# A four-layer graph network on one core: f2's column computed inside the values' matmuls, its maximum taken through a 32x32 transpose, and ScalarE's work in layer 0 in another order

## The reference

```
layer 0, 3 (GAT):  Wh = h @ W;  f1 = Wh @ a1;  f2 = Wh @ a2
                   e[n,m] = leaky_relu(f1[n] + f2[m], 0.2), masked; softmax over m
                   out = elu(attention @ Wh) in layer 0, relu(...) in layer 3
layer 1:           a softmax per channel over the neighbours, weights from softplus(h)
layer 2:           4 heads: scores h_head @ h_head.T, masked softmax, times h_head;
                   then one such attention on the joined heads, leaky_relu, layernorm
```

## Time and profile before

| what | value |
|---|---|
| median of 3 runs | 1895.6 us (1892.89 to 1895.61) |
| the profiled execution | 1894.35 us, its span 1892.1 us |
| busy in the span | PE 97%, PEld 81%, DVE 88%, ACT 68%, POOL 48% |
| layer 0 | about 31 to 245 us of the span |
| layer 1 | about 245 to 406 us |
| layer 2 | about 406 to 1731 us (the first units of layer 3 lie inside its end) |
| layer 3 | to the end |

### The profile page before, as it was taken

How to read it: one execution, slowest core, us unless ns; L and a number is a source line. 1 busy time by engine, 2 the same in 40 slices (tenths; PEclk the granted TensorE clock), 3 DMA queues, 4 the chain that set the end, 5 groups by cost and what they waited for, 6 DMA issues and landing times.

```text
span 1892.1 us, 92007 instructions
## 1 busy us (share of the span) xinstructions
PE 1840.0 (97%) x42280; PEld 1531.0 (81%) x42280; DVE 1660.6 (88%) x1932; ACT 1285.1 (68%) x2052; POOL 907.5 (48%) x686
## 2 busy tenths in 40 slices
PE   7999899999999999999999999999999999999998
PEld 6887799987878788787888878878787878877887
DVE  6989899768898889988899888989988899888998
ACT  4998676446777777777777777777777777754332
POOL 6888999633233343424344342443334334264753
PEclk8999999999999999999999999999999999999999
DMA  7000000012111112221111211111111112201111
GB/s 192 4 4 4 3 2 3 2 25 36 37 36 36 36 36 37 34 38 31 36 34 35 38 34 36 36 36 36 36 37 36 36 35 32 42 3 26 26 32 31
DMA packets 134321, 61.02 MB, mean 32 GB/s; under 512 B 122416, under 2 KB 122672, under 8 KB 133936
## 3 DMA queue, kind: packets, MB, share of 16 engines
q1 hardware_dynamic: 131712, 54.55, 14.3%
q10 hardware_dynamic: 2224, 0.59, 0.1%
HBM read 8.98 MB, written 4.19 MB: 7 GB/s over the span
## 4 chain that ended last, share of the span: by engine, by line
PE 84%; POOL 8%; DVE 4%; issue 2%; ACT 1%; DMA 0%; ACTq 0%; POOLq 0%; DVEq 0%
PE ACC L1914 30%; PE S L1895 29%; PE S L1872 8%; PE ACC L1712 7%; PE AX L1957 3%; PE AX L1930 2%; DVE ring L1336 1%; PE AX L1702 1%; PE AX L1692 1%; POOL above L643 1%; PE S L1769 1%; POOL o L639 1%; DVE ring L1484 1%; PE AX L1753 1%; POOL X L649 1%
## 5 line engine op out<-in xcount | busy, mean ns | idle before, releaser
L1484 DVE TENSOR_TENSOR ring<-ring,mask_self_t 128x1024 f32<-128x1024 f32 x640 | 878.0, 1385 | 68.8 <-ACT ring L1092 61.1
L1092 ACT ACTIVATE ring<-S,dot_bias 128x1024 f32<-128x1024 f32 x640 | 711.5, 1113 | 274.3 <-PE S L1895 235.7
L1914 PEld LDWEIGHTS ACC<-V,ring 128*64 128x64 f32 x20480 | 706.7, 138 | 109.8 <-issue 13.2
L1914 PE MATMUL ACC<-V,ring 128*64 128x65 f32 x20480 | 708.0, 222 | 0.0
L1895 PE MATMUL S<-FA 128*64 128x512 f16 x5120 | 665.5, 380 | 1.1 <-ACT ring L1092 0.9
L1895 PEld LDWEIGHTS S<-FA 128*64 128x64 f16 x5120 | 268.6, 110 | 141.8 <-issue 10.9
L1336 DVE SCALAR_TENSOR_TENSOR ring<-S,pair_q,mask_t 128x1024 f32<-128x1024 f32 x256 | 313.9, 1273 | 16.5 <-issue 4.3
L1712 PEld LDWEIGHTS ACC<-V,ring 128*64 128x64 f32 x8192 | 253.3, 139 | 56.2 <-DVE ring L1336 34.7
L1712 PE MATMUL ACC<-V,ring 128*64 128x65 f32 x8192 | 270.4, 225 | 20.3 <-DVE ring L1336 11.5
L819 POOL TENSOR_TENSOR EV_both<-score,recip 128x512 f32<-128x512 f32 x64 | 96.8, 1512 | 263.9 <-DVE score L1494 263.8
L1872 PE MATMUL S<-parts,mask_t 128*128 128x128 bf16 x3072 | 173.8, 220 | 4.7 <-DVE o L1461 3.5
(11 more groups left out here) (149 smaller groups left out, 2076.6 us busy)
## 6 DMA issues: line engine op xcount, KB each, us to landing
FA<-FA SPq DMA_DIRECT2D x160, 128.0 KB, 2.3
X<-in_x SPq DMA_DIRECT2D x16, 256.0 KB, 4.8
ring<-in_adj SPq DMA_DIRECT2D x8, 512.0 KB, 8.1
out_x<-X SPq DMA_DIRECT2D x16, 256.0 KB, 2.6
FA<-HL SPq DMA_TRANSPOSE x80, 3.1
wh<-in_wh_t ACTq DMA_DIRECT2D x2, 64.0 KB, 6.5
bh_bc<-in_bh ACTq DMA_DIRECT2D x1, 128.0 KB, 9.9
w_gat<-in_w_gat ACTq DMA_DIRECT2D x4, 16.0 KB, 3.9
```

The lines of the kernel that those rows point to most:

```text
L1092: act.activation(ring[:, jt, :], S[jt % 2][:, :], ACT.Exp, bias=dot_bias[:, n % 2:n % 2 + 1])\
L1484: dve.tensor_tensor(ring[:, jt, :], ring[:, jt, :], mask_self_t[:, jt, :], ALU.mult)\
L1914: last = pe.matmul(acc_of(t)[rows, :], ring[:, jt, t * P + c * CUT:t * P + (c + 1) * CUT], V[:, n % 3, jt, 1:D + 2], start=(jt == 0 and t ...
```

## The change

Seven things are changed.

1. `w_gat` holds W a2, then W, then W a1. One group of matmuls of 65 columns for each tile gives f2 and the values together (`gat_columns`); `gat_peak` and its 32 instructions a unit are gone. The group stands where `gat_peak` stood: for unit cur+2, after tile 2 of cur.
2. ScalarE copies the 65 columns to V (`gat_columns` on ScalarE), now for unit cur+2. V has four buffers in place of three. VectorE's `node_max` waits for this copy and reads f2 from V, no longer from PSUM.
3. The maximum over partitions starts with a 32x32 block transpose on VectorE: f2 and norm2 are 32 columns wide, of which 8 are used; copy, transpose, maximum over 32 columns, each waiting for the one before. So only 32 partitions' values need to be spread: the two matmuls of `spread` have 32 columns in place of 128, and `node_peak` and `bias` read 32 in place of 128. This holds for layer 0, 2 and 3 (`norms` and `bias` too).
4. A round of ScalarE in layer 0 becomes: copy ACC of cur-1, h_relu of cur+2, exponents and gain of cur+1, columns of cur+2, late_shifts, gat_below of cur-1, late_squares.
5. For the last two graphs of layer 0 the ELU is max(exp(min(o,0))-1, o): GpSimd makes the minimum, ScalarE one exponent in place of two passes, VectorE one instruction (`gat_elu`), GpSimd adds once in place of twice.
6. In layer 3 the same order without the means; the two buffers of the first three units are chosen anew.
7. Three memsets and one wait at the start, and four small copies of `w_gat` in place of two.

The diff, cut to its core:

```diff
+    SQ = 32
...
-        V = sb("V", [P, 3, T, D + 2])
+        V = sb("V", [P, 4, T, D + 2])
...
-            return 2 * ((b + layer // 3) % 2)
+            return (0, 1, 2)[b % 3] if layer == 0 else (2, 3, 0)[b % 3]
...
+        ELU_SWITCH = B - 2
...
# GpSimd
+                if layer == 0 and b >= ELU_SWITCH:
+                    wait(pool, elu_made, b)
+                    pool.wait_ge(gat_o, n + 1)
+                    pool.tensor_scalar(below[:, :], o[:, :], 0.0, None, ALU.min).then_inc(elu_below, 1)
...
+                if layer == 0 and b >= ELU_SWITCH:
+                    pool.wait_ge(elu_made, b + 1)
+                    pool.tensor_tensor(x_of(b), x_of(b), tiles(o[:, :]), ALU.add).then_inc(x_done[layer], 1)
...
# ScalarE
-                act.activation(halves_of(V[:, buf, :, 1:D + 1]), V_FULL, ACT.Copy).then_inc(gat_v_copied, 1)
+                act.activation(halves_of(V[:, buf, :, 0:D + 1]), V_GAT, ACT.Copy).then_inc(gat_v_copied, 1)
...
                     for k in steps_beside(cur):
                         channel_argument(k, k % 2)
+                    if cur + 1 < B:
+                        gat_factors(layer, cur + 1)
+                    if cur + 2 < B:
+                        gat_columns(layer, cur + 2)
                     if late_stats(layer, cur) is not None:
                         late_shifts(late_stats(layer, cur))
-                    if cur + 1 < B:
-                        gat_factors(layer, cur + 1)
...
# VectorE
-                dve.tensor_copy(f2[:, par, :].rearrange("p (h t) -> p h t", h=2), AX_both[:, :, 0:T // 2])\
-                    .then_inc(f2_copied, 1)
-                dve.tensor_reduce(f2_max[:, :], AX_both[:, :, 0:T // 2], mybir.AxisListType.XY, ALU.max).then_inc(f2_maxed, 1)
-                dve.wait_ge(f2_maxed, n + 1)
+                dve.wait_ge(gat_v_copied, n + 1)
...
+                dve.tensor_copy(f2[:, par, 0:T], V[:, gat_buf(layer, b), :, 0]).then_inc(f2_copied, 1)
+                dve.wait_ge(f2_copied, n + 1)
+                dve.transpose(f2_turned[:, :], f2[:, par, :]).then_inc(f2_across, 1)
+                dve.wait_ge(f2_across, n + 1)
+                dve.tensor_reduce(f2_max[:, :], f2_turned[:, :], AX_X, ALU.max).then_inc(f2_maxed, 1)
...
-                dve.tensor_reduce(f2_peak[:, par:par + 1], AX[k][:, 0:P], AX_X, ALU.max).then_inc(f2_peaked, 1)
+                dve.tensor_reduce(f2_peak[:, par:par + 1], AX[k][:, 0:T * P // SQ], AX_X, ALU.max).then_inc(f2_peaked, 1)
...
+            def gat_elu(b):
+                dve.wait_ge(elu_exp, b + 1)
+                dve.scalar_tensor_tensor(out=o[:, :], in0=below[:, :], scalar=-1.0, in1=o[:, :],
+                                         op0=ALU.add, op1=ALU.max).then_inc(elu_made, 1)
...
-                dve.tensor_reduce(norm2_max[:, :], norm2[:, :], AX_X, ALU.max).then_inc(bound_dve, 1)
+                dve.transpose(norm2_turned[:, :], norm2[:, :]).then_inc(bound_dve, 1)
+                dve.wait_ge(bound_dve, n + 2)
+                dve.tensor_reduce(norm2_max[:, :], norm2_turned[:, :], AX_X, ALU.max).then_inc(bound_dve, 1)
...
-                dve.tensor_reduce(norm2_all[:, :], AX[k][:, 0:P], AX_X, ALU.max).then_inc(ax_free[k], 1)
+                dve.tensor_reduce(norm2_all[:, :], AX[k][:, 0:T * P // SQ], AX_X, ALU.max).then_inc(ax_free[k], 1)
...
# TensorE
-                    last = pe.matmul(AX[k][c * CUT:(c + 1) * CUT, 0:P], column.broadcast_to([P, CUT]), ident[:, :],
-                                     start=True, stop=True, skip_group_check=True)
+                    last = pe.matmul(AX[k][c * CUT:(c + 1) * CUT, 0:T * P // SQ], column.broadcast_to([P, CUT]),
+                                     turned_cols(ident[:, :]), start=True, stop=True, skip_group_check=True)
...
                     gat_sums(layer, cur, jt)
                     if jt == 0 and cur + 1 < B:
-                        gat_nodes(layer, cur + 1)
+                        gat_gain(layer, cur + 1)
                     if jt == 2 and cur + 2 < B:
-                        gat_peak(layer, cur + 2)
+                        gat_columns(layer, cur + 2)
```

More of the change, by code:

```diff
@@ L378, in place_norm, with place_columns, place_nodes @@
             place(("T", layer, b), 1)
-        def place_peak(layer, b):
-            place_f2(layer, b)
-            place_bias(layer, b)
         def place_bias(layer, b):
             place(("GN", layer, b), 0)
-        def place_f2(layer, b):
-            for half in range(2):
-                place(("GF", layer, b, half), half)
-        def place_nodes(layer, b):
+        def place_columns(layer, b):
             for half in range(2):
                 place(("GV", layer, b, half), half)
+        def place_nodes(layer, b):
+            place_columns(layer, b)
+            place_bias(layer, b)
         def place_first_layer():
             place_norm(0, 0)
-            place_peak(0, 0)
             place_nodes(0, 0)
             place_norm(0, 1)
-            place_peak(0, 1)
+            place_nodes(0, 1)
             place_norm(0, 2)
@@ L410, in place_beside @@
         def place_beside(layer, cur):
-            if cur + 1 < B:
-                place_nodes(layer, cur + 1)
             if cur + 2 < B:
-                place_peak(layer, cur + 2)
+                place_nodes(layer, cur + 2)
             if cur + 3 < B:
@@ L463, in gnn_stack @@
         place_norm(3, 3)
-        place_nodes(3, FIRST)
         place_values(LAST)
         place_bound(LAST)
-        place_peak(3, FIRST + 1)
-        place_norm(3, FIRST + 2)
-        for cur in range(FIRST, B):
-            if cur > FIRST:
-                place_beside(3, cur)
-            else:
-                place_nodes(3, cur + 1)
-                place_peak(3, cur + 2)
-                place_norm(3, cur + 3)
+        for cur in range(FIRST - 1, B):
+            place_beside(3, cur)
         def stats_before(layer):
@@ L989, in gat_layer @@
                 h_relu(0, 0)
-                for t in range(2, 5):
-                    mask_copy(t)
+                mask_copy(2)
                 gat_columns(0, 0)
+                mask_copy(3)
+                mask_copy(4)
+                gat_exponents(0, 0)
                 mask_copy(5)
@@ L1239, in last_layer @@
                         gat_factors(3, cur + 1)
+                    if cur + 2 < B:
+                        gat_columns(3, cur + 2)
                 gat_sums(3, B - 1)
@@ L1416, in gat_layer @@
                                 channel_part(k, k % 2, (1, 3, 6, 7).index(jt))
+                        if jt == 7 and cur > ELU_SWITCH:
+                            gat_elu(cur - 1)
             def channel_step(k, par):
@@ L1424, in channel_step @@
                 channel_part(k, par, 3)
+                if k == 0:
+                    gat_elu(B - 1)
                 channel_result(k, par)
@@ L1723, in gat_sums, with gat_columns @@
                 weigh(tile_of(layer, b, jt), jt, V[:, buf, jt, 0:D + 1])
-            def gat_peak(layer, b):
+            def gat_columns(layer, b):
                 w = layer // 3
                 pe.wait_ge(h_ready, H0[layer] + b + 1)
-                for half in range(2):
-                    take_bank(AX_AT["GF", layer, b, half])
-                for t in range(T // 2):
-                    for half in range(2):
-                        for c in range(2):
-                            last = pe.matmul(AX[half][c * CUT:(c + 1) * CUT, t:t + 1], node_tiles(b, t, half, c),
-                                             w_gat[half * D:(half + 1) * D, w, D + 1:D + 2], start=True, stop=True,
-                                             skip_group_check=True)
-                        if t == T // 2 - 1:
-                            last.then_inc(ax_full[half], 1)
-            def gat_nodes(layer, b):
-                gat_columns(layer, b)
-                gat_gain(layer, b)
-            def gat_columns(layer, b):
-                w = layer // 3
                 for half in range(2):
```

121 lines of the change are left out of this document (65 added, 56 removed).

## The result

The changed kernel takes 1922.8 us (median of 4 runs, 1920.9 to 1923.4); the kernel before took 1895.6 us beside it. The ratio is 1.0144, with a 95% interval of 1.0131 to 1.0156. The forecast was 1900.0 us, in a range of 1887 to 1907: the direction was right, the size was not. The profiled execution has a span of 1918.9 us, 26.8 more than before, and that is what the traces must account for.

What follows compares the result with a forecast made beforehand. TensorE carried 84% of the chain of waits; in layer 0 the order within a round decides. Layer 0 +6.3, layer 2 +1.0, layer 3 -2.9 make +4.4 on 1894.35, 1898.8; median 1.25 higher: 1900.0 us, range 1887 to 1907.

Steps and rivals of the forecast that it cites:

- The loop is 12.41 us: Layer 0: TensorE's 5.48 us and ScalarE's 6.93 form a closed loop that sets each round, above GpSimd's 11.49.
- the copy to V 0.58; the eight shifts 1.93: Layer 0, ScalarE's part of the loop: these two, ELU passes 1.20, squares and what follows 3.22, together 6.93 us.
- 9.3: Layer 0, rounds 1 to 11: eleven rounds lose 0.84 us each to the new loop, +9.3 us.
- Rival 2: Layer 0's new loop does not bind, rounds stay with GpSimd at 11.49 us: 1890.7 us, chance 0.16.
- -3.3: Tail of layer 0, after round 11: shorter path to the exponents and less GpSimd work, -3.3 us, bounds 0 and -5.
- +0.3: Start of layer 0: f2 passes over ScalarE, but unit 0's values no longer wait: +0.3 us, between -0.5 and +1.5.
- the spread's gain of 0.15: Layer 2, TensorE: each of 80 spreads of 0.22 us gets 0.15 shorter with a quarter of the columns.
- +0.11: Layer 2, per graph of five units: 0.29 + 0.12 - 0.30 us, from late spreads against shorter ones.
- the longer `node_max` (copy, transpose, maximum) takes back 0.05 to 0.1: Layer 3, VectorE's loop: the longer chain takes this many us from savings of 0.12 on spread and 0.10 on peak.
- The wider copy, the 65th column, four buffers and memsets cost nothing: Values' group is bound by 32 weight loads, ScalarE has idle time in layer 3; without that cover, 0.01 us each.
- the 1.7: Layer 3: each of 13 units gains 0 to 0.2 us, taken as 0.13, in all -1.7 us.
- Rival 3: Small VectorE steps cost more (transpose and waits 0.35): layer 2 +6, layer 3 near 0, about 1908 at most; chance 0.14.

Runs made afterwards that it cites:

- its one variant: The kernel before with the spread of norm_max one source tile later, behind tile 6 instead of 5: 1892.3 us, ratio 0.9986.
- the square: Layer 2 graph times, old or transposed norm chain, spread behind tile 5 or 6: old 80.61 and 80.41 us, transposed 80.83 and 79.77.
- with one input: The changed kernel with f2's copy from SBUF made by a tensor_reduce over an axis of one element: 1911.1 us, ratio 1.0084.
- The one-edit runs: Changed kernel with 32 filler matmuls before tile 0, 1915.9 us; ScalarE's wait and bank release behind the shifts, 1914.7; f2 copied by a one-element reduction, 1911.1.

## Why the prediction was right and wrong

The direction was right, and the time was 22.8 us above the forecast. Three costs that the sum left out make most of it: VectorE's copy of f2 that now reads SBUF (10.4 us, taken as nothing), TensorE's lower clock in layer 0 (7.1, in no term) and ScalarE's wait for its own copy (3.9, in no term).

**Layer 0's order: right mechanism, term too small.** "The loop is 12.41 us" was right in its mechanism: with the clock and the wait taken away it is 12.48. That it is so near is partly luck, as the gain took 0.16 more than its row and the copy to V, without the wait, 0.08 less. The step that failed is the list of what stands on ScalarE, "the copy to V 0.58; the eight shifts 1.93". The copy is followed by a wait for itself, and the shifts start 0.84 us after it. In the earlier trace rows the wait could not be seen, since the next instruction stood 0.69 us for GpSimd anyway; but the wait stands in the code, and the row of L915 there shows 0.17 us behind h_relu from the same cause. Without the wait the shifts start 0.50 us after the copy, so it costs 0.35 a round, 3.9 us. That the wait was also there before, hidden, is read from the code and not tested. The second missing term is the clock, 7.1 us: I forecast that TensorE would stand before its first tile and priced the standing at its own length, with all durations taken from rows at a granted clock of 1.00. The rest, some 2 us (22.1 - 9.3 - 3.9 - 7.1), is several small things: rounds 1 and 11, with 13.50 and 13.35 us, are together 1.2 above a settled round, 12.48 is 0.07 a round above 12.41, round 10 is 0.3 longer; against this the eleventh round of before was already 12.42 us, where I had reckoned with 11.57. It wasn't followed further. Rival 2 (the loop does not bind) is refuted.

**Start and tail.** -3.3 was -2.7 and +0.3 was +1.1, within their bounds. The start says little: the single traces of the kernel before and of its one variant have 44.01 and 43.49 us, and the changed kernel with a later spread, whose start is the same program, 45.43 in place of 45.10; with the old norm chain it is 46.08. Layer 1's -1.6 was in no term.

**Layer 2: right, with one wait missed.** The transpose at 0.20 took 0.21, the spread's gain of 0.15 was 0.13, and the 15 graphs together +1.8 where my sum had +1.6. The per-graph sum of +0.11 was +0.22 in the settled graphs: a third spread of each graph had come to wait for its maximum, 46 of 80 in place of 30, which I had not counted. The first two graphs were faster than before and hide a third of this in the sum. That the whole edit then brings nothing was the point of the step, and the square shows why: the gain is there and the wait eats it. What I did not draw from it is that the wait could be had back by a later place in TensorE's program.

**Layer 3: wrong in sign.** The step was "the longer `node_max` (copy, transpose, maximum) takes back 0.05 to 0.1", and with it "The wider copy, the 65th column, four buffers and memsets cost nothing". The transpose and the maximum cost what I said. The copy of f2 had moved from PSUM to SBUF, and I took its old price with it. That one move costs 7.5 us over 13 units (150.06 against 142.61 with one input), and 2.9 in the stretch ahead of them. Without it the 13 units are 0.9 us faster than before, the sign forecast and half of the 1.7; a settled unit takes 10.73 us, 0.17 less than before, where I had 0.13. The stretch ahead, forecast at -1.2, is -3.4 without the move. Rival 3, small VectorE steps that cost more, named the engine, but bounded the excess at 0.08 a step and put it on the transpose; the copy cost up to 1.08 more.

**What of the 27.2 us is shown.** The one-edit runs give 7.1 for the clock, 3.9 for ScalarE's wait and 10.4 for the copy (7.5 and 2.9). The loop itself stands in the sum as forecast, 9.3: no run isolates it, but with the old place of the shifts all of layer 0's 22.1 us are gone. These make 30.7. The start, the rest of layer 0's rounds and 15 graphs of layer 2 add 4.7 (1.1 + 1.8 + 1.8); the tail, layer 1, the stretch ahead of layer 3's 13 units and these units, both without the copy's cost, give back 8.6 (2.7 + 1.6 + 3.4 + 0.9). That is 26.8, the difference of the two spans.

## What to carry to other kernels

- When an operand moves from PSUM to SBUF, or back, price the instruction anew: a VectorE copy or scaling from SBUF to SBUF, or one with two SBUF inputs, can last until the end of a large GpSimd instruction with two inputs beside it. Look in the trace for small instructions of one line with durations far apart; a reduction over one element is a copy that does not wait.
- When a new order makes TensorE stand once a round, its later instructions may become dearer too. Price the standing and a lower clock behind it as two terms, and keep long work of ScalarE whose result is not needed soon (here the means) out of the stretch that TensorE waits for.
- When an edit shortens one engine's work and lengthens the chain that feeds it, test it together with a later place for the consumer: each edit alone gave 0 to 3 us in layer 2, both together some 15.

## What the runs showed of the hardware

- VectorE's copy of 128x8 fp32 values took 0.16 us or anything up to 1.24 us, ending 0.03 us behind the GpSimd TENSOR_TENSOR of 128x512 values under way. The same with two SBUF inputs; never with one input and no copy, nor from PSUM. Beside GpSimd's TENSOR_SCALAR of 1.92 us the same copy took 0.16 or 0.17 us, eleven times.
- The granted clock was 1.00 and 0.88 in neighbouring rounds with the same work and the same 1.9 us of standing. What decides in which round it falls isn't settled by these runs.
- Waiting for its own copy cost ScalarE 0.35 us (0.84 against 0.50 from start to start), more than the 0.24 us of idle time that the wait's row names: the next instruction otherwise starts 0.10 us before the copy ends.
- A 32x32 block transpose of 128x32 fp32 values took 0.21 us on VectorE, the maximum over 32 columns 0.19, and the four instructions of two spreading matmuls some 0.13 us less at 32 columns than at 128.
- Behind a PSUM copy and two releases VectorE stood 0.25 us before the dependent transpose; behind a PSUM read without releases 0.03 us.
